# Gated unit begun before the attention layer ahead of it is finished, and an output bias added by VectorE

## The chip, the cores and the metric

The kernel runs on one core of a Trainium2 chip. The metric is the device time of one execution in microseconds (us). The core has five engines that run side by side and wait for one another through semaphores: TensorE (PE in the rows, its weight loads PEld), VectorE (DVE), ScalarE (ACT), GpSimd (POOL) and SyncE (SP), which here only issues DMAs. A name with a q (DVEq, PEldq, SPq) is the engine's sequencer.

## The reference, cut to what matters

Four layers work on a stream x of 2 batches x 512 tokens x 256 channels, in float32. Each layer adds a gated cross-attention and then a gated feed-forward part to x:

```python
x = x + tanh(g_xattn[l]) * attention_l(layernorm(x), ctx)      # l = 0..3
x = x + tanh(g_ffn[l]) * feed_forward_l(layernorm(x))
# attention of l = 2 and 3 ends with:   o @ Wo + bo
# feed-forward of l = 2, the gated unit:
h = silu(x @ w1 * s1) * (x @ w2 * s2)                          # 256 -> 1024
h = gelu(h @ h1 * sh1); h = gelu(h @ h2 * sh2)                 # 1024 -> 1024
out = h @ w3 * s3                                              # 1024 -> 256
```

Attention l = 1 has no biases. Feed-forward 1 is a mixture of 8 experts. The change is in attention 2 and 3 and in the gated unit.

## The kernel before, in words

The program is written engine by engine; each engine runs its list in order, and every dependence between engines is a `wait_ge` on a semaphore.

**Attention.** `schedule(l)` (line 144) writes one list of steps, which all engines walk through, each doing its own part. A group is two heads of one batch: 16 groups in layers 1 and 2, 8 in layer 3, the first half of them batch 0. A step "max" is a product whose row maximum VectorE takes (lines 1502 and 2217); "score" gives the transposed scores (L1521), which ScalarE turns into exponentials (L1176); "values" multiplies them with the values (L1536); "context" turns the sums back (L1555) and they are divided. The maxima run ahead of the scores, so near the end of a layer VectorE is through with them while TensorE and ScalarE still have scores to do. There batch 0 is finished: "heads" turns its context (L1563, one for every 128 channels: two in layer 2, one in layers 1 and 3), VectorE copies it out of PSUM (L2254), "out" multiplies two token tiles with Wo (L1574) and adds the bias bo by a product of a row of ones with the one row of bo (L1576), and VectorE adds that to x (L2261). Statistics (L1820, L1825), GpSimd's reciprocal deviation (L847, L848) and VectorE's normalisation (L1840) follow for batch 0. After the last scores "tokens" turns batch 0's normalised tiles (L1292), "heads" turns batch 1's context, ScalarE copies it (L1192), and "out" follows for batch 1. `bo` was replaced beforehand by bv @ Wo + bo (L1624, L1625, L1207).

**Between attention 2 and the gated unit.** TensorE runs 22 products that nobody reads (`hold_clock(LN_HOLDS[5], 2)`, L1283), then the transposes of batch 1 (L1292), then waits until ScalarE has copied them (`ln_evac`, L961). Two flags tell whether any weight of the unit needs a second float32r part; each of TensorE and VectorE reads them (`value_load`, L1778 and L2489) and branches (`If`, L1779, L2490, L2495). VectorE reads them right after its last maximum, and all its later steps of attention 2 stand within the two branches. There too it converts the unit's first two weight chunks (`split_weights`, L2443) behind the "out" steps, and splits the tokens of both batches in two float32r parts (`split_tokens`, L2420 and L2421).

**The gated unit** (`gated_unit`) is run once for batch 0 and once for batch 1. Its first layer has 8 blocks f of 128 channels: 8 products per block (L1729), ScalarE's silu (L1252), VectorE's multiplication (L2474) and conversion (L2476), GpSimd's low part (L932). Block f waits for the conversion of block f - 2 (`gated_high`). The second layer waits for the low parts of all blocks (`act_split`). The weights go by chunks over two buffers; SyncE loads a further chunk once VectorE has converted one (L584). Layer 3's attention follows, then the last feed-forward part, whose products begin with L1796.

## Time and profile before

| | us |
|---|---|
| median of 3 runs (lowest to highest) | 1114.46 (1112.02 to 1122.93) |
| the profiled execution, its own time | 1117.24 |
| its span, first to last instruction | 1115.5 |
| TensorE busy in it | 1015.7 |
| VectorE busy in it | 770.4 |
| mean granted clock of TensorE | 0.939 |

The span is what the trace covers; the execution's own time is 1.7 us longer. Busy time of TensorE counts an instruction at its modelled length, so it says that the engine had work and not that it ran at its best rate. The clock column gives the share of 2.4 GHz that TensorE was granted: 1.00 is 2.4 GHz and 0.50 is 1.2 GHz.

### The profile page before, as it was taken

The page shows a single profiled execution, that of the slowest core. Times are in us where ns is not written, and L with a number is a line of the kernel's source. Part 1 is how long each engine was busy: PE and PEld are TensorE (multiplying, and loading weights), DVE is VectorE, ACT ScalarE, POOL GpSimd, SP SyncE. Part 2 cuts the span into 40 slices and gives each one's busy share as a digit, 9 for nine tenths or more (in the row PEclk, how much of TensorE's full clock was granted, in tenths as well). Part 3 has the DMA queues.
Part 4 walks back from the last instruction along what each step waited for, and adds up shares of the span by engine and source line. Part 5 has one row for each costly group of instructions (what it writes and reads, how often), then busy time and mean ns, then how long its engine had stood idle before and what let it go on. Part 6 is the DMA issues. An engine that isn't in the chain of part 4 may idle for free.

```text
span 1115.5 us, 17599 instructions
## 1 busy us (share of the span) xinstructions
PE 1015.7 (91%) x6606; PEld 596.7 (53%) x6606; DVE 770.4 (69%) x1465; ACT 485.6 (44%) x704; POOL 287.3 (26%) x439
## 2 busy tenths in 40 slices
PE   8888975999999969995899999998989999899998
PEld 4323353544444446995454444444778787644445
DVE  5879868899999451453699999923545654799636
ACT  2553331477777700110157777732312212367542
POOL 3545700133433211003123443220400500114200
PEclk9889976999999968998999999969999999999889
DMA  6688912103330604985412241001254242100011
GB/s 208 216 280 277 354 31 65 40 24 110 116 91 13 171 28 165 357 323 144 139 40 65 50 122 44 24 2 38 95 170 132 95 140 72 35 12 13 2 29 38
DMA packets 79185, 121.86 MB, mean 109 GB/s; under 512 B 9733, under 2 KB 52904, under 8 KB 79090
## 3 DMA queue, kind: packets, MB, share of 16 engines
q1 hardware_dynamic: 59278, 79.29, 23.2%
q10 hardware_dynamic: 19044, 39.22, 10.1%
q0 software_dynamic: 768, 2.10, 0.6%
q8 instruction: 58, 0.95, 0.4%
q14 instruction: 37, 0.30, 0.1%
HBM read 92.10 MB, written 27.81 MB: 107 GB/s over the span
## 4 chain that ended last, share of the span: by engine, by line
PE 71%; DVE 20%; issue 4%; ACT 2%; POOL 1%; DMA 1%; SPq 0%; DVEq 0%; ACTq 0%; POOLq 0%
PE bank L1536 14%; PE bank L1502 14%; PE bank L1729 11%; DVE arena L2217 9%; PE st_bank L1656 4%; PE bank L1668 4%; PE st_bank L1521 3%; PE bank L1304 2%; PE st_bank L1729 2%; PE bank L1574 2%; PE st_bank L1454 1%; PE st_bank L1283 1%; PE st_bank L1292 1%; PE bank L1576 1%; PE bank L1555 1%
## 5 line engine op out<-in xcount | busy, mean ns | idle before, releaser
L2217 DVE TENSOR_REDUCE arena<-bank 128x1 f32<-128x512 f32 x640 | 396.8, 680 | 35.4 <-PE bank L1502 34.4
L1176 ACT ACTIVATE arena<-st_bank 128x1024 f32<-128x1024 f32 x320 | 312.2, 1022 | 155.4 <-PE st_bank L1521 154.4
L1502 PE MATMUL bank<-g_a 64*128 64x512 f32 x480 | 181.4, 477 | 11.4 <-DVE arena L2217 3.0
L1536 PE MATMUL bank<-arena,vaug 128*9 128x256 f32 (+2 forms) x2560 | 171.0, 385 | 2.0 <-ACT arena L1176 2.0
L1502 PEld LDWEIGHTS bank<-g_a 64*128 64x128 f32 x480 | 73.2, 183 | 124.5 <-DVE arena L2217 100.0
L1729 PE MATMUL bank<-g_a,g_w 128*128 128x512 f32 x512 | 119.3, 394 | 4.3 <-DVE g_w L2443 3.2
L1521 PE MATMUL st_bank<-g_a 64*128 64x512 f32 x480 | 117.4, 425 | 0.0
L1729 PEld LDWEIGHTS bank<-g_a,g_w 128*128 128x128 f32 x512 | 97.0, 190 | 25.9 <-DVE g_w L2443 3.6
L899 POOL COPY arena<-arena 8x32 f32<-8x32 f32 x160 | 32.1, 200 | 260.5 <-issue 137.0
L1536 PEld LDWEIGHTS bank<-arena,vaug 128*9 128x9 f32 (+2 forms) x2560 | 56.1, 92 | 77.4 <-issue 40.7
L1502 PE MATMUL bank<-g_x,g_a 64*128 64x512 f32 x160 | 63.5, 494 | 9.9 <-DVE arena L2217 3.6
L1521 PEld LDWEIGHTS st_bank<-g_a 64*128 64x128 f32 x480 | 63.2, 188 | 7.6 <-issue 4.2
L1254 ACT ACTIVATE arena<-bank,arena 128x512 f32<-128x512 f32 x32 | 22.0, 688 | 96.6 <-PE bank L1729 96.6
L2420 DVE CAST g_a<-arena 128x512 fp32r<-128x512 f32 x32 | 13.7, 427 | 65.6 <-ACT arena L1254 65.6
L847 POOL TENSOR_SCALAR rstd<-mv 128x4 f32<-128x4 f32 x16 | 3.8, 239 | 205.8 <-DVE mv L1825 205.8
L913 POOL TENSOR_TENSOR arena<-arena,minus_one 128x16 f32<-128x16 f32 x17 | 49.3, 2899 | 11.7 <-ACT arena L1169 11.7
L1217 ACT ACTIVATE arena<-st_bank 128x352 f32<-128x352 f32 x32 | 14.8, 464 | 85.8 <-PE st_bank L1656 85.8
L1502 PEld LDWEIGHTS bank<-g_x,g_a 64*128 64x128 f32 x160 | 26.1, 190 | 46.8 <-DVE arena L2217 32.6
L961 ACT ACTIVATE xnT<-st_bank 128x512 f32<-128x512 f32 x24 | 13.0, 594 | 85.8 <-PE st_bank L1292 85.8
L932 POOL TENSOR_TENSOR g_a<-arena,g_a 128x512 fp32r<-128x512 f32 x16 | 23.7, 1483 | 92.0 <-DVE g_a L2476 92.0
L1283 PE MATMUL st_bank<-identb 128*128 128x512 bf16 x149 | 40.5, 437 | 7.2 <-DVE arena L2330 5.0
L1656 PE MATMUL st_bank<-arena 128*128 128x176 f32 x256 | 41.2, 321 | 0.7 <-DVE arena L2346 0.7
(314 smaller groups left out, 1507.4 us busy)
## 6 DMA issues: line engine op xcount, KB each, us to landing
arena<-in_glu_w SPq DMA_DIRECT2D x39, 512.0 KB, 3.3
arena<-kv_table SPq DMA_DIRECT2D x11, 1024.0 KB, 7.9
ctxT<-in_glu_w ACTq DMA_DIRECT2D x22, 512.0 KB, 6.3
arena<-in_w SPq DMA_DIRECT2D x20, 512.0 KB, 6.0
kparts<-arena ACTq DMA_DIRECT2D x12, 512.0 KB, 5.1
arena<-in_w ACTq DMA_DIRECT2D x12, 512.0 KB, 3.6
xnT<-kv_table SPq DMA_DIRECT2D x5, 1024.0 KB, 6.9
g_a<-kparts SPq DMA_DIRECT2D x24, 192.0 KB
```

The costliest lines, as they stand in the source:

```text
L899: ch.link(pool.tensor_copy(mxq[0:HG * QT, r * SQ:(r + 1) * SQ], mxt[gi % 2][r * SQ:r * SQ + HG * QT, :]))
L913: ch.link(pool.tensor_tensor(rsum_p, sums[:, :, :, dh], bc(minus_one[:, 0:1].unsqueeze(2), [P, QT, 2 * HG]), ALU.pow))
L932: pool.tensor_tensor(g_a[0][1][:, f, :], g_tmp[f % 2], g_a[0][0][:, f, :].bitcast(F32), ALU.subtract).then_inc(act_split, 1)
L1176: act.activation(prob[sl % PROBS], st_bank[sl % 2][:], ACT.Exp, scale=scale).then_inc(exp_ready, 1)
L1283: pe.matmul(bank[b], identb[:], bc(identb[:].unsqueeze(1), [P, CH // P, P]), start=True, stop=True)
L1502: pe.matmul(bank[TURN_BANKS[place % 3]], Qc[gi % KQ_BUFS][rows, qt * P:(qt + 1) * P], Kc[gi % KQ_BUFS][rows, half * CH:(half + 1) * CH], s ...
L1521: ins = pe.matmul(st_bank[sl % 2][:, hh, :], Kc[gi % KQ_BUFS][rows, kt * P:(kt + 1) * P], Qc[gi % KQ_BUFS][rows, :], start=True, stop=True)
L1536: ins = pe.matmul(bank[7][at:at + dh + 1, 0:D], vaug[l][:, b * KT + 2 * m + i, h0 + hh, :], tiles[:, a], start=(m == 0 and i == 0), stop=( ...
L1656: ins = pe.matmul(bank[i % 4][:, f % UP_PER_BANK * CAP:(f % UP_PER_BANK + 1) * CAP], mw1[wbuf][:, c, f * P:(f + 1) * P], unit_inT[n % 2][: ...
L1668: ins = pe.matmul(bank[4 + n % 2][:, c * CAP:(c + 1) * CAP], mw2[wbuf][:, f, c * P:(c + 1) * P], hid[n % 2][:, f, :], start=(f == 0), stop ...
L1729: ins = pe.matmul(out, stationary, moving, start=(first and i == 0), stop=(last and i == len(pairs) - 1))
L2217: dve.tensor_reduce(mxh[gi % 2][:, col, hf:hf + 1], bank[TURN_BANKS[place % 3]], AX.X, ALU.max).then_inc(max_red, 1)
```

## The change

1. On VectorE the reading of the flags and the branch stand after batch 0 of attention 2 has been normalised, and no longer after the last maximum. In the branch stand, in this order: the first two weight chunks, the last context's division, `split_tokens(0)`, the "out" steps of batch 1, the statistics, block 0 of the unit, the normalisation of batch 1, block 1, and so on; `split_tokens(1)` stands behind block 3.
2. TensorE goes from the last "out" step straight to the unit's block 0, without the 22 holding products; the transposes of batch 1 stand ahead of block 3 and go to banks 4 and 5.
3. ScalarE copies batch 0's turned tokens ahead of the last "heads", loads the table of silu (by an activation of one element) before the unit, and copies batch 1's turned tokens ahead of block 3.
4. The bias: at the mixture's start TensorE spreads the two rows bo over 128 partitions, ScalarE multiplies them with tanh(g_xattn) into `bias_rows`, and in layers 2 and 3 VectorE adds that row to all of x (128x2048) behind batch 0's "heads" copies. The bias products of "out" are gone.

```diff
-LN_HOLDS = {3: 8, 4: 16, 5: 22, 7: 16}
+LN_HOLDS = {3: 8, 4: 16, 7: 16}
+SECOND_TOKENS_AT, SECOND_BANKS = 3, 2
...
@@ scalar, attention(l)
+                    elif step[0] == "tokens" and l == 2:
+                        ln_evac(2 * l + 1, [step[1]])
@@ scalar, ahead of the mixture
+            act.wait_ge(prepv_mm, NCT + 2)
+            for l in (2, 3):
+                ins = act.activation(bias_rows[:, l - 2], bank[3][:, (l - 2) * D:(l - 1) * D], ACT.Copy, scale=tgx[:, l:l + 1])
+            ins.then_inc(prepv_evac, 1)
@@ scalar, gated unit
-            ln_evac(5)
+            act.activation(exp_ready_table[:], onesf[0:1, 0:1], ACT.Silu)
...
+                if (h, layer, f) == (0, 0, SECOND_TOKENS_AT):
+                    ln_evac(5, [1], SECOND_BANKS)
@@ tensor, output
-                            ins = pe.matmul(o, xnT[0:n, c, t * P:(t + 1) * P], w[l]["o"][:, c, :], start=(c == 0), stop=(c == EC[l] - 1 and l == 1))
-                        if l > 1:
-                            ins = pe.matmul(o, onesf[0:1, :], w[l]["bo"][:], start=False, stop=True)
+                            ins = pe.matmul(o, xnT[0:n, c, t * P:(t + 1) * P], w[l]["o"][:, c, :], start=(c == 0), stop=(c == EC[l] - 1))
@@ tensor, the mixture's start
+            for l in (2, 3):
+                ins = pe.matmul(bank[3][:, (l - 2) * D:(l - 1) * D], onesf[0:1, :], w[l]["bo"][:], start=True, stop=True)
+            ins.then_inc(prepv_mm, 1)
...
+            pe.wait_ge(prepv_evac, NCT + 2)
             pe.wait_ge(slots_ready, 1)
@@ tensor, behind attention(2)
-            hold_clock(LN_HOLDS[5], 2)
-            ln_transposes(5, [1])
-            pe.wait_ge(xnT_ready, (LN_AT[5] + 1) * 4)
@@ tensor, gated_unit
+                            if (h, f) == (0, SECOND_TOKENS_AT):
+                                ln_transposes(5, [1], SECOND_BANKS)
...
+                        if (h, layer, f) == (0, 1, 0):
+                            pe.wait_ge(xnT_ready, (LN_AT[5] + 1) * 4)
@@ vector, attention(l)
+                        if l > 1 and c == EC[l] - 1:
+                            dve.wait_ge(prepv_evac, NCT + 2)
+                            ch.link(dve.tensor_tensor(x[:], x[:], bc(bias_rows[:, l - 2].unsqueeze(1), [P, NT, D]), ALU.add))
@@ vector, ahead of the branch
-            all_maxima = second.index(("shift", NGROUPS[2] - 1)) + 1
-            attention(2, second[:all_maxima])
+            first_done = second.index(("normalise", 0)) + 1
+            last_context = next(i for i, step in enumerate(second) if step[:2] == ("normal", NGROUPS[2] - 1)) + 1
...
+            attention(2, second[:first_done])
@@ vector, gated_unit
-                normalise(5, first=1)
+                attention(2, second[first_done:last_context])
                 split_tokens(0)
-                split_tokens(1)
+                attention(2, second[last_context:])
+                tile_statistics(5, NT - 1)
...
+                            if a == 1:
+                                normalise_batch(5, 1)
+                            if a == SECOND_TOKENS_AT + 1:
+                                split_tokens(1)
@@ vector, both branches
-                attention(2, second[all_maxima:])
                 gated_unit(True)
```

VectorE behind its last maximum of attention 2, before and after (STREAM_TRANSPOSE ends the maxima, COPY xnT is the "heads" copy of L2254):

```order
L2229 STREAM_TRANSPOSE arena<-arena 128x32 [waits max_lo,max_fin]
L2489 TENSOR_LOAD low_flags
L2489 ISA x2
L2489 TENSOR_LOAD low_flags
L2489 ISA x2
L2490 COMPARE_AND_BRANCH
L2254 COPY xnT<-bank 128x512 [waits ctxT_mm] x2
L2261 SCALAR_TENSOR_TENSOR x<-bank,tgx,x 128x512 [waits out_mm]
```

```order
L2241 STREAM_TRANSPOSE arena<-arena 128x32 [waits max_lo,max_fin]
L2266 COPY xnT<-bank 128x512 [waits ctxT_mm] x2
L2269 TENSOR_TENSOR x<-x,wo 128x2048 [waits prepv_evac]
L2276 SCALAR_TENSOR_TENSOR x<-bank,tgx,x 128x512 [waits out_mm,chain_dve]
```

The five rows of flags and branch left this place, and the 128x2048 addition (wo is the buffer of `bias_rows`) came behind the copies; flags and branch now stand behind the four normalisations of batch 0.

VectorE from batch 1's "out" steps on, after the change (CAST g_x and the TENSOR_TENSOR g_x behind it are `split_tokens`, L2496 and L2498 are a block's multiplication and conversion):

```order
L2276 SCALAR_TENSOR_TENSOR x<-bank,tgx,x 128x512 [waits out_mm]
L1832 BN_STATS bnst<-x 128x6 [waits x_ready] x3
L1837 BN_AGGR mv<-bnst 128x2 [waits chain_dve]
L1837 BN_AGGR mv<-bnst 128x2 x3
L2496 SCALAR_TENSOR_TENSOR arena<-st_bank,arena 128x512 [waits glu_act,glu_ld]
L2498 CAST g_a<-arena 128x512 [waits chain_dve]
L1852 TENSOR_SCALAR xn<-x,mv,rstd 128x256 [waits rstd_ready,var_ready]
L1852 TENSOR_SCALAR xn<-x,mv,rstd 128x256 x3
L2496 SCALAR_TENSOR_TENSOR arena<-st_bank,arena 128x512 [waits glu_act]
L2498 CAST g_a<-arena 128x512 [waits chain_dve]
```

Before, the two weight chunks, the normalisation and all four token splits stood between the statistics and block 0's multiplication; now the statistics are followed by block 0, and the normalisation stands between blocks 0 and 1.

TensorE from the last "out" step to the unit, before and after (L1737 is the unit's product of L1729):

```order
L1576 MATMUL bank<-bo,onesf 128x256
L1283 MATMUL st_bank<-identb 128x512 x22
L1292 MATMUL st_bank<-ident,xn 128x128 [waits xn_ready]
...
L1778 TENSOR_LOAD low_flags [waits xnT_ready]
...
L1779 COMPARE_AND_BRANCH
L1729 MATMUL st_bank<-g_x,g_w 128x512 [waits tokens_split,glu_split]
```

```order
L1584 MATMUL bank<-wo,xnT 128x256 [waits ctxT_ready]
L1584 MATMUL bank<-wo,xnT 128x256 x3
L1790 TENSOR_LOAD low_flags
...
L1791 COMPARE_AND_BRANCH
L1737 MATMUL st_bank<-g_x,g_w 128x512 [waits tokens_split,glu_split]
L1737 MATMUL st_bank<-g_x,g_w 128x512 x15
L1737 MATMUL st_bank<-g_x,g_w 128x512 [waits gated_high,tokens_split,glu_split]
L1737 MATMUL st_bank<-g_x,g_w 128x512 x7
L1302 MATMUL bank<-ident,xn 128x128 [waits xn_ready]
```

The 22 holding products are gone, and the transposes of batch 1 moved from ahead of the unit to behind its block 2.

## Rows read from the trace of the kernel before

**Rows 1.** The page: busy time, share of the span and instructions of each engine.

```profile
PE 1015.7 (91%) x6606; PEld 596.7 (53%) x6606; DVE 770.4 (69%) x1465; ACT 485.6 (44%) x704; POOL 287.3 (26%) x439
```

**Rows 2.** Chain of waits, 722 to 800 us: start us, us, what.

```profile
726.30 0.21 DVE arena L2229
...
727.62 2.76 issue
...
731.81 2.08 PE bank L1574 x4
...
761.05 1.09 ACT xnT L1192 x2
...
763.94 1.06 PE bank L1574 x4
765.00 0.62 PE bank L1576 x2
...
769.11 0.75 DVE x L2261
...
770.52 1.19 DVE g_w L2443 x2
...
772.93 1.05 POOL rstd L848
...
774.08 1.38 DVE xn L1840 x4
...
787.12 0.70 ACT arena L1252
787.84 0.76 DVE arena L2474
788.63 0.44 DVE g_a L2476
...
799.44 1.67 POOL g_a L932
```

**Rows 3.** Stretches: start:end, length, busy us (instructions) by engine, TensorE's clock, DMA.

```profile
369.70:373.20 3.50, 3.50 (x29) 1.85 (x27) 1.18 (x2) 1.94 (x3) 3.23 (x3) 1.00 0.05 5
1052.00:1063.00 11.00, 11.00 (x56) 5.12 (x54) 3.60 (x11) 3.07 (x3) 3.95 (x4) 0.53 0.01 2
731.90:748.00 16.10, 16.10 (x48) 7.96 (x48) 3.29 (x10) 2.05 (x2) 0.74 (x3) 0.50 0.00 0
```

**Rows 4.** Timelines of DVE and PE, ends of attention 1 and 3: start, length, instruction, idle.

```profile
368.41 0.21 DVE L2229 STREAM_TRANSPOSE arena<-arena 128x32 f32<-128x32 f32 x1
386.00 0.66 PE L1555 MATMUL bank<-ident,xnT 128*128 128x128 f32 x4 [0.50 <-ACT xnT L1188]
1049.31 0.21 DVE L2229 STREAM_TRANSPOSE arena<-arena 128x32 f32<-128x32 f32 x1
1073.49 0.66 PE L1555 MATMUL bank<-ident,xnT 128*128 128x128 f32 x4 [0.50 <-ACT xnT L1188]
```

**Rows 5.** Timeline of PE, attention 2's last context and the unit's first products.

```profile
758.89 0.66 PE L1555 MATMUL bank<-ident,xnT 128*128 128x128 f32 x4 [0.50 <-ACT xnT L1188]
...
778.58 5.52 PE L1729 MATMUL st_bank<-g_x,g_w 128*128 128x512 f32 x16 [2.63 <-DVE g_x L2421]
784.99 3.96 PE L1729 MATMUL st_bank<-g_x,g_w 128*128 128x512 f32 x16 [0.89 <-DVE g_a L2476]
...
801.15 26.18 PE L1729 MATMUL bank<-g_a,g_w 128*128 128x512 f32 x114 [0.55 <-POOL g_a L932]
```

**Rows 6.** Lines L2421 and L2368, all instructions: min/median/max ns.

```profile
L2421 DVE TENSOR_TENSOR g_x<-xnT,g_x x4: 691/692/692, 775.8 to 779.0; 128x512 fp32r<-128x512 f32 x4
L2368 DVE TENSOR_TENSOR ctxT<-ctxT x21: 1212/1225/1227, 443.5 to 508.4; 128x1024 int32<-128x1024 int32 x21
```

**Rows 7.** Chain of waits, end of attention 3; then PE's timeline at the mixture's start.

```profile
1078.56 0.43 PE bank L1576 x2
...
415.62 12.40 PE L1283 MATMUL st_bank<-identb 128*128 128x512 bf16 x44 [4.97 <-DVE arena L2330]
```

More of the change, by code:

```diff
@@ L342, in build @@
         exp_ready_table = sb("exp_ready_table", [1, 1])
+        bias_rows = wo0[:]
         chain_dve, chain_act, chain_pool = sem("chain_dve"), sem("chain_act"), sem("chain_pool")
@@ L956, in _, with ln_evac @@
             ch = Chain(act, chain_act)
-            def ln_evac(stage, halves=range(2)):
+            def ln_evac(stage, halves=range(2), first=0):
                 for i in (h * DC + c for h in halves for c in range(DC)):
@@ L960, in ln_evac @@
                     act.wait_ge(xnT_mm, LN_AT[stage] * 4 + i + 1)
-                    act.activation(xnT[:, c, h * CH:(h + 1) * CH], bank[i], ACT.Copy).then_inc(xnT_ready, 1)
+                    act.activation(xnT[:, c, h * CH:(h + 1) * CH], bank[first + i], ACT.Copy).then_inc(xnT_ready, 1)
             def ctx0_evac(b):
@@ L1291, in transposes @@
                     for c in range(ec):
-                        ins = pe.transpose(bank[(t // QT) * ec + c][0:n, (t % QT) * P:(t % QT + 1) * P], src[:, t, c * P:c * P + n], ident[:])
+                        ins = pe.transpose(bank[base + (t // QT) * ec + c][0:n, (t % QT) * P:(t % QT + 1) * P], src[:, t, c * P:c * P + n], ident[:])
                         if t % QT == QT - 1:
@@ L1443, in _, with ln_transposes @@
             i8_products(0)
-            def ln_transposes(stage, batches=range(B)):
-                transposes(xn, xnT_mm, 0, D, xn_ready, XN0[stage], batches)
+            def ln_transposes(stage, batches=range(B), first=0):
+                transposes(xn, xnT_mm, first, D, xn_ready, XN0[stage], batches)
             def query_product(l, j, parts=range(DC)):
@@ L2495, in _ @@
             with dve.If(no_low):
-                attention(2, second[all_maxima:])
                 gated_unit(False)
```

1 line of the change is left out of this document (added).

## The prediction

> **What bounds the kernel now.** I read the page first: TensorE is busy for 91% of the span and VectorE for 69% [rows 1]. An engine as full as that gains from what it no longer does, from what it no longer waits for, and from its clock. So next came the chain of waits around the change, 722 to 800 us, then the clock of stretches, then the timelines. They show three things.
>
> First, behind its last maximum (the transpose at 726.30) VectorE does not copy batch 0's context, although that is turned; the branch stands in between, and 2.76 us go by in which nothing is waited for [rows 2]. TensorE's first output product starts only at 731.81. From 731.90 to 748 TensorE is busy all the time, but at 1.2 GHz, clock 0.50 [rows 3]: four products with Wo take 2.08 us, and 1.06 us in batch 1, at full clock [rows 2]. Layer 1 has the same transition without branch and without bias, and its clock stays at 1.00 [rows 3].
>
> Second, between the last output product (over at 769.1) and the unit's steady rhythm TensorE does nothing that counts: holding products, transposes of batch 1, then 2.63 us of waiting for VectorE's token split, then two blocks at a lower rate (5.52 us where the next two take 3.96) [rows 5]. VectorE's own work in that stretch (weights, statistics, normalisation, splits) is a chain that nothing covers [rows 2].
>
> Third, the second layer starts at 801.15, when GpSimd has made the last low part [rows 2, 5]; from there TensorE runs almost without a gap. Whatever earlier start that point gets moves all that is behind it.
>
> **Part A, the end of attention 2.** From the last transpose of maxima to the turning of the last context: 758.89 - 726.30 = 32.6 us in layer 2 [rows 2, 5], but 386.00 - 368.41 = 17.6 in layer 1 [rows 4], with the same number of groups. The changed layer 2 differs from layer 1 in one more "heads" (about 0.6 with its copy) and in 8 more products with Wo, 2 x 1.06 = 2.1 [rows 2]. That makes 20.3, so A gives 32.6 - 20.3 = 12.3 us: the stall, the biases (four at half clock) and the half clock itself. It holds only if the clock stays up, as in layer 1. VectorE reads the flags later, in time in which it waits for the last context: it normalises batch 0 some 13 us behind the copies, loads and branch take 4, the two weight chunks 1.2, and the last context comes 20.3 us behind the transpose. About 2 us are left over; if they were not enough, the excess would be paid in full.
>
> The branch is the first place where I weigh a page. The row shows 2.76 us between the branch and the next work [rows 2]. The Trainium skill (Advanced Engine Details and Errata, Control Flow Timing) gives a compare-and-branch about 108 ns. By the page, moving it would return almost nothing and A would be some 2.7 us smaller; the measurement decides, and I keep the row.
>
> **Part B, batch 1's output.** Four bias pieces of 0.62 us go [rows 2]: 2.5 us. ScalarE now copies the turned tokens before the turned context. The two context copies took 1.09 us and started as soon as TensorE had turned the first half; the token copies are two of the same size and can start some 0.65 us earlier, so the context is late by about 0.45. B = 2.05 us.
>
> **Part C, from the last output product to the second layer.** Before: 801.15 - 769.1 = 32.0 us. After, counted from the end of the output products (time 0), with 1.98 us for a block [half of 3.96, rows 5], 0.70 for silu, 0.76 and 0.44 for multiplication and conversion [rows 2]:
> TensorE does blocks 0 and 1 from 0 to 4.0. VectorE finishes output and statistics at 2.3 (from 769.11 to GpSimd's row at 772.93, less the chunks' 1.19 and 0.3 for its shorter first instruction [rows 2]); GpSimd's deviation is there 1.4 later. Block 0 is converted at 4.0, normalisation (1.38) ends at 5.4, block 1 is converted at 6.6, a weight chunk ends at 7.3. Block 2 runs 4.1 to 6.1, the 8 transposes to 7.0, block 3 from 7.0 to 9.0, block 4 to 11.0, block 5 from 11.1 to 13.1. VectorE converts block 3 at 10.95, a weight chunk ends at 11.65, and then `split_tokens(1)` takes 2 x (0.42 + 0.69) = 2.2 (0.69 [rows 6]), to 13.85. Only then does block 4's multiplication come, converted at 15.1, for which block 6 waits: TensorE idles 2.1 us. Blocks 6 and 7 end at 19.2, silu and VectorE at 21.2, GpSimd's low part (1.67 [rows 2]) at 22.9. C = 32.0 - 22.9 = 9.1 us. Its parts: the wait and the holding products 9.5, the silu table that is loaded ahead 1.3, the slow first blocks 1.6, less transposes 0.9 and the new stall 2.1; they make 9.4, near enough. Queued behind `split_tokens(1)` on VectorE are the multiplications of blocks 4 to 7, and TensorE waits for them through the conversions; behind the normalisation it is block 1's multiplication, which costs nothing because block 2's product covers it.
>
> **Part D, the end of attention 3.** The same stretch lasts 1073.49 - 1049.31 = 24.2 us [rows 4]; with layer 1's 17.6 (one "heads", one set of products, as in layer 1) the most to gain is 6.6. There the clock falls without any stall: 0.53 from 1052 to 1063 [rows 3], behind output products with 32 rows and biases with one. If it still falls, only the four biases go, 0.43 each at full clock [rows 7] and twice that for the two at half: 2.6 us. Nothing in the trace shows products of 32 rows without the biases between them. I take the middle, 4.6, and keep both ends.
>
> **Part E, layer 3's last output.** Four biases of 0.43 us [rows 7] = 1.7, of which VectorE's two additions and the holding products behind them may keep some; bounds 0 and 1.7, taken 1.3.
>
> **Costs taken as nothing.** The addition to x over 2048 columns stands in no row. 512 columns take 0.69 us and 1024 take 1.22 [rows 6], so 0.53 per 512 more: 2.3 us; bounds 1.2 and 4 x 0.69 = 2.8. In layer 2 it lies in the 2.8 us between the copies and the end of the first output step. In layer 3 the first addition of output starts 0.9 us behind its product, but no later than before, and its bank is wanted three turns on. The spreading of the bias (four products of one row, about 2.1 us at half clock, two small activations) lies in the 4.97 us that TensorE waits for VectorE ahead of the 44 holding products [rows 7]; bounds 0 and 0.5, since a load of ScalarE's queue goes out 4 us later.
>
> **Sum.** 12.3 + 2.05 + 9.1 + 4.6 + 1.3 = 29.4 us. Against the execution's own time: 1117.24 - 29.4 = 1087.9. The median of the runs is 2.8 us lower, which gives 1085.1. I say 1086.5.
>
> **Rivals.**
> 1. The clock falls inside the unit. VectorE's queue makes TensorE idle for 2.1 us at block 6, and a wait of 2.63 us together with transposes stood ahead of the slow blocks [rows 5]. For it: that row; against it: the new idle time has dense products on both sides. Price once: 5.52 - 3.96 = 1.6, twice 3.2. Time 1088 to 1090. This is also where the Trainium skill speaks against the change (TensorE: Matmul & The Clock Gate, Part 4, PE-mode transpose): transposes do not count as busy time for the clock. By that rule the eight transposes that now stand within the blocks, followed by the wait at block 6, pull the clock down. In attention 2's last part the rows of before show transposes with the clock still at 1.00 afterwards (1.06 us for four products at 763.94 [rows 2]), which neither proves nor refutes it.
> 2. Attention 2's output of batch 0 stays at half clock: the stall was not the reason, the transposes ahead of it were. Then 4.2 us of products with Wo, 0.9 of scores and 1.0 to 1.4 of values are paid twice, A shrinks by 6.5, and the time is 1093. Against it: layer 1.
> 3. VectorE becomes the bound of the unit's first layer: normalisation, splits and chunks are only moved, and each second block waits for product and silu (2.7 us) as block 0 does. VectorE's own work behind the last product is about 18.3 us; with 4 x 2.7 that is 29.1 instead of 22.9: C is 2.9, time 1093. If all eight wait, 39.9, and 1103.5: the early start is given back whole.
> 4. Slower than before. Half clock can last under full load: 16.1 us of it with TensorE busy throughout [rows 3]. If the many small waits of the unit's first layer leave TensorE at 1.2 GHz for the first batch's pass, its 16 us of blocks and 16 x 16 dense products at 0.23 us (26.18 / 114 [rows 5]) = 59 us are paid twice: 1086.5 + 75 = 1161. It decides from 29.4 us of dense work at half clock on, about 128 products. Against it: at 784.99 the clock was back, four blocks' time after the unit's start [rows 5].
> That the change does not do what it says would be case 3 in its whole form.
>
> **How the numbers follow.** Forecast (own range 1080 to 1089, by D's ends of +-2 and some 2 us of run to run difference) 0.62; rival 1, 0.13; rival 2, 0.11; rival 3, 0.11; rival 4, 0.03. What a measurement of this kernel can tell from no change is about 1%, 11 us. The range 1079 to 1097 takes in the forecast, rivals 1 and 2 and the near form of rival 3, and leaves out the far form of rival 3 and rival 4. Faster by over 1% (under 1103.3): 0.95; within 1%: 0.02, from the far end of rival 3; slower: 0.03.
>
> **What would show it.** Right: the first product with Wo of attention 2's batch 0 about 3 us behind the last transpose of maxima and at clock 1.00; 20 us from that transpose to the last context's turning; the unit's first block directly behind the last output product, 4.0 us for two; one gap of about 2 us ahead of block 6; 23 us from the last output product to the second layer; 18 to 22 us for the stretch in layer 3; an addition over 2048 columns of 2.3 us, twice. Wrong: a clock of 0.50 in the first 16 us behind the transpose, gaps ahead of most blocks, the last context's division waiting for the branch, or the unit's dense products at 0.43 us each.

## The result, and the profile after

| | before | after |
|---|---|---|
| median of the runs beside each other (lowest to highest) | 1114.05 (1112.02 to 1122.93) | 1084.69 (1080.08 to 1086.85) |
| the profiled execution, its own time | 1117.24 | 1080.08 |
| its span | 1115.5 | 1078.3 |
| TensorE busy | 1015.7 | 985.0 |
| VectorE busy | 770.4 | 776.8 |
| mean granted clock | 0.939 | 0.956 |

The ratio of the times is 0.9716, with a 95% interval from 0.9655 to 0.9777. The median is 29.4 us lower, and the sum on record said 29.4. That agreement is partly luck: one term was 2.9 us too large, the other four were too small by 0.5 to 1.9, and part of the gain belongs to something that the kernel before does in some executions and not in others. One run of this study, of e6 below (1121.30 us at a clock of 0.848), was a slow one and is left out of its median and ratio.

To compare, I cut each execution at the same six instructions: VectorE's last transpose of maxima in attention 2 (the last of that layer), TensorE's turning of the last context, VectorE's last addition of attention 2's output, the first product of the unit's second layer behind GpSimd's last low part, the last transpose of maxima in attention 3, the turning of its last context, and the end of the span. A, B, C, M, D, E are the stretches between them. Here are A to C in the chain of waits of the changed kernel, columns as in [rows 2]:

```profile
723.99 1.92 PE bank L1584 x8
725.91 0.43 PE st_bank L1531
726.34 1.93 PE bank L1584 x8
...
740.24 0.66 PE bank L1565 x4
740.90 0.78 PE st_bank L1302 x7
741.70 1.09 ACT xnT L963 x2
742.78 0.99 ACT xnT L1196 x2
743.82 3.73 PE bank L1584 x16
747.65 0.75 DVE x L2276
...
751.65 2.34 DVE xn L1852 x4
...
759.88 1.44 DVE g_x L2437
...
764.37 5.34 PE st_bank L1737 x16
...
771.75 1.67 POOL g_a L934
773.46 2.60 PE bank L1737 x10
```

The last transpose of maxima stands at 720.64, so A is 740.24 - 720.64 = 19.6 us. The "issue" piece of [rows 2] (time in which VectorE waits for nothing that the profile shows) is gone from the chain, eight products with Wo take 1.92 us (at half clock four took 2.08), and the unit's products follow the last output directly. Against [rows 3], the windows of the same two stretches read, in the changed kernel:

```profile
724.00:740.00 16.00, 15.09 (x146) 7.39 (x146) 7.46 (x17) 10.38 (x13) 3.82 (x4) 1.00 0.12 37
762.00:764.30 2.30, 0.00 (x0) 0.00 (x0) 2.23 (x6) 0.18 (x1) 0.00 (x1) 0.92 0.24 96
764.40:770.00 5.60, 5.60 (x19) 4.48 (x20) 3.21 (x5) 0.95 (x2) 2.96 (x3) 0.74 0.28 97
1021.00:1038.00 17.00, 15.94 (x164) 6.90 (x162) 7.42 (x16) 12.50 (x16) 8.33 (x9) 1.00 0.01 1
```

The columns are the stretch, its length, busy time of PE, PEld, DVE, ACT and POOL with their instructions, the granted clock, the DMA share and GB/s. The first and the last row show the end of attention 2 and of attention 3 at full clock. The two rows between show the price inside the unit: TensorE has nothing to do for 2.3 us of this window while VectorE is busy for 2.23 of them, and in the 5.6 us behind it the clock is 0.74.

The timeline of the changed kernel, first where VectorE reads the flags, then in the unit (start, duration, instruction, in brackets the idle time ahead of it and what ended it):

```profile
736.30 1.30 DVE L2460 CAST g_w<-arena 128x1024 fp32r<-128x1024 f32 x2 [2.86 <-issue]
740.94 0.26 DVE L2250 RECIPROCAL arena<-bank 128x16 f32<-128x16 f32 x1 [3.34 <-PE bank L1565]
...
751.59 1.29 POOL L934 TENSOR_TENSOR g_a<-arena,g_a 128x512 fp32r<-128x512 f32 x1
751.65 2.34 DVE L1852 TENSOR_SCALAR xn<-x,mv,rstd 128x256 f32<-128x256 f32 x4
...
755.17 6.28 PE L1737 MATMUL st_bank<-g_x,g_w 128*128 128x512 f32 x24 [0.55 <-DVE g_a L2498]
...
759.35 1.68 POOL L934 TENSOR_TENSOR g_a<-arena,g_a 128x512 fp32r<-128x512 f32 x1 [0.82 <-DVE g_a L2498]
...
759.79 1.52 DVE L2437 CAST g_x<-xnT 128x512 fp32r<-128x512 f32 x1
...
761.95 0.42 DVE L2437 CAST g_x<-xnT 128x512 fp32r<-128x512 f32 x1
...
764.37 5.33 PE L1737 MATMUL st_bank<-g_x,g_w 128*128 128x512 f32 x16 [2.91 <-DVE g_a L2498]
...
773.46 1.90 PE L1737 MATMUL bank<-g_a,g_w 128*128 128x512 f32 x7 [0.55 <-POOL g_a L934]
```

The 2.86 us of the branch are still there, but VectorE then waits another 3.34 us for the last context, so nobody waits for it. The gap ahead of block 6 is 2.91 us (2.1 were forecast), and the two blocks behind it take 5.33 us and not 3.96. Of two equal conversions in the token split, the one that begins 0.44 us behind a subtraction of GpSimd takes 1.52 us, and the one without such a neighbour 0.42. The normalisation, which took 1.38 us before [rows 2], takes 2.34 beside another such subtraction.

### The profile page after: what moved, and what is told of

It reads as the page before. It is cut to its first block, busy times and chain, and to the rows that moved or that the text cites. A ratio compares the mean times of both kernels' runs of the same rounds, so it can differ in the third digit from the quotient of the medians.

```text
span 1078.3 us, 17505 instructions
## 1 busy us (share of the span) xinstructions
PE 985.0 (91%) x6556; PEld 582.9 (54%) x6556; DVE 776.8 (72%) x1467; ACT 486.8 (45%) x707; POOL 290.1 (27%) x439
## 4 chain that ended last, share of the span: by engine, by line
PE 70%; DVE 21%; issue 4%; ACT 2%; POOL 2%; DMA 1%; SPq 0%; POOLq 0%; DVEq 0%; ACTq 0%
PE bank L1546 14%; PE bank L1512 14%; PE bank L1737 12%; DVE arena L2229 9%; PE st_bank L1667 4%; PE bank L1679 4%; PE st_bank L1531 3%; PE bank L1314 2%; PE st_bank L1737 2%; PE st_bank L1464 1%; PE bank L1584 1%; PE st_bank L1302 1%; PE bank L1565 1%; DVE bnst L1832 1%; DVE arena L1961 1%
## 5 line engine op out<-in xcount | busy, mean ns | idle before, releaser
L1546 PE MATMUL bank<-arena,vaug 128*9 128x256 f32 (+2 forms) x2560 | 168.5, 381 | 2.0 <-ACT arena L1178 2.0
L1737 PE MATMUL bank<-g_a,g_w 128*128 128x512 f32 x512 | 117.7, 390 | 4.3 <-DVE g_w L2460 3.2
L1531 PE MATMUL st_bank<-g_a 64*128 64x512 f32 x480 | 115.2, 417 | 0.0
L1737 PEld LDWEIGHTS bank<-g_a,g_w 128*128 128x128 f32 x512 | 95.8, 188 | 25.5 <-DVE g_w L2460 3.6
L901 POOL COPY arena<-arena 8x32 f32<-8x32 f32 x160 | 34.7, 217 | 257.9 <-issue 137.1
L1512 PEld LDWEIGHTS bank<-g_x,g_a 64*128 64x128 f32 x160 | 26.1, 191 | 45.8 <-DVE arena L2229 31.9
L881 POOL MEMSET g_a<- 2x512 f32 x56 | 28.9, 516 | 46.5 <-PE st_bank L1531 44.2
```

Source lines behind the costliest of these rows:

```text
L881: ins = pool.memset(Qc[gi % KQ_BUFS][h * HALF_P:h * HALF_P + SHIFT_ROWS].bitcast(F32), 0.0)
L901: ch.link(pool.tensor_copy(mxq[0:HG * QT, r * SQ:(r + 1) * SQ], mxt[gi % 2][r * SQ:r * SQ + HG * QT, :]))
L1512: pe.matmul(bank[TURN_BANKS[place % 3]], Qc[gi % KQ_BUFS][rows, qt * P:(qt + 1) * P], Kc[gi % KQ_BUFS][rows, half * CH:(half + 1) * CH], s ...
L1531: ins = pe.matmul(st_bank[sl % 2][:, hh, :], Kc[gi % KQ_BUFS][rows, kt * P:(kt + 1) * P], Qc[gi % KQ_BUFS][rows, :], start=True, stop=True)
L1546: ins = pe.matmul(bank[7][at:at + dh + 1, 0:D], vaug[l][:, b * KT + 2 * m + i, h0 + hh, :], tiles[:, a], start=(m == 0 and i == 0), stop=( ...
L1737: ins = pe.matmul(out, stationary, moving, start=(first and i == 0), stop=(last and i == len(pairs) - 1))
```

## The experiments

Twelve runs were made beside the pair above: eight altered kernels (e1 to e8) and four repeats (c1 to c4). This table has the stretches of each in its profiled execution, in us, from the starts of the rows named above, and the median of its timed executions with the ratio to the kernel before, timed beside it on the same chip (there its median was 1109.55 to 1114.05). For the three kernels whose second layer starts without a gap behind a low part, C and M are given as their sum.

| kernel | A | B | C | M | D | E | median | ratio (95% interval) |
|---|---|---|---|---|---|---|---|---|
| before | 32.6 | 10.2 | 32.0 | 248.2 | 24.2 | 42.0 | 1114.05 | |
| c2, before again | 24.8 | 10.2 | 31.7 | 246.9 | 19.4 | 42.1 | 1102.81, one run | |
| c3, before a third time | 32.8 | 10.2 | 32.0 | 248.1 | 24.2 | 42.1 | 1111.69, one run | |
| e1, branch only | 22.5 | 10.2 | 32.9 | 248.2 | 19.4 | 41.7 | 1101.04 | 0.9915 (0.9881 to 0.9949) |
| e2, bias only | 23.5 | 7.1 | 32.7 | 246.5 | 17.7 | 40.1 | 1092.12 | 0.9838 (0.9811 to 0.9864) |
| c4, bias only again | 23.4 | 7.1 | 32.9 | 246.9 | 17.7 | 40.2 | 1097.23, one run | |
| e3, changed, no bias part | 22.5 | 10.5 | 26.0 | 248.2 | 19.4 | 42.0 | 1091.94 | 0.9839 (0.9803 to 0.9876) |
| changed | 19.6 | 7.4 | 25.8 | 246.9 | 17.7 | 40.2 | 1084.69 | 0.9716 (0.9655 to 0.9777) |
| c1, changed again | 19.6 | 7.4 | 25.9 | 247.9 | 17.7 | 40.2 | 1083.21 | 0.9749 (0.9712 to 0.9786) |
| e8, no table ahead | 19.6 | 7.4 | 27.1 | 246.9 | 17.7 | 40.1 | 1083.40 | 0.9753 (0.9718 to 0.9789) |
| e4, late token split | 19.6 | 7.4 | 21.7 | 248.0 | 17.7 | 40.2 | 1079.19 | 0.9715 (0.9686 to 0.9743) |
| e5, low parts left out | 19.6 | 7.4 | C + M 273.7 | | 17.7 | 40.3 | 1083.28 | 0.9735 (0.9698 to 0.9773) |
| e6, last low part by VectorE | 19.6 | 7.4 | C + M 269.2 | | 17.7 | 40.1 | 1078.11 | 0.9695 (0.9662 to 0.9727) |
| e7, third layer's weights | 19.6 | 7.4 | C + M 262.3 | | 17.7 | 40.2 | 1071.08 | 0.9642 (0.9609 to 0.9675) |

A to E agree within 0.1 to 0.3 us wherever nothing was changed and the clock was the same. What lies ahead of A does not: the last transpose of maxima in attention 2 stands between 719.7 and 728.4 us over these kernels, although hardly anything before it differs. Most of this spread arises early: attention 1's last transpose of maxima already stands between 362.9 and 370.7 us. That is why the profiled pair differs by 37.2 us and the medians by 29.4: 726.30 - 720.64 = 5.7 us came from ahead of the change. For terms of one or two microseconds the stretches are the better measure, and the times serve for the sums.

**Branch alone (e1) and bias alone (e2).**

```diff
-            all_maxima = second.index(("shift", NGROUPS[2] - 1)) + 1
+            all_maxima = second.index(("normalise", 0)) + 1
```

> The kernel before, with VectorE's reading of the flags and its branch moved behind the normalisation of attention 2's batch 0, and nothing else: the bias products, the holding products and the whole way into the unit stay. Theory (the stall takes the clock down in attention 2): the four products with Wo of batch 0 take 1.06 us and no longer 2.08, the stretch from the last transpose of maxima to the last context's turning falls from 32.6 to 22 to 23 us, layer 3 stays at 24.2 us, and the time is about 1104 us. Rival (the bias products take it down, as they may in layer 3): the clock still reads about 0.5 from 732 to 748, only the stall of 2.76 us goes, the stretch lasts 29 to 30 us and the time is about 1111.

In e2 the kernel before takes the whole of point 4 of the change, with the same lines as the diff shown above, and nothing of points 1 to 3:

```diff
+                        if l > 1 and c == EC[l] - 1:
+                            dve.wait_ge(prepv_evac, NCT + 2)
+                            ch.link(dve.tensor_tensor(x[:], x[:], bc(bias_rows[:, l - 2].unsqueeze(1), [P, NT, D]), ALU.add))
...
-                        if l > 1:
-                            ins = pe.matmul(o, onesf[0:1, :], w[l]["bo"][:], start=False, stop=True)
```

> The kernel before, with the output bias added by VectorE in attention 2 and 3 (the rows spread at the mixture's start, the bias products gone), and nothing else: flags and branch, holding products and the way into the unit stay. Theory (two separate causes): the stall of 2.76 us stays and takes attention 2's clock down as before, so that its stretch falls from 32.6 only to about 29.5 us; batch 1's output gains 2.5, and layer 3's stretch goes from 24.2 to 17.6 because its clock stays at 1.00, its last output gains 1.3 to 1.8. Time about 1100 us. Rival (the biases alone take down the clock in attention 2): its stretch falls to about 23 us and the time is about 1094. Rival for layer 3 (its clock held in the changed kernel for another reason): its stretch stays at 21.6 us or more and the time is about 1104.

The first output products in e1's timeline, then in e2's:

```profile
728.02 1.13 PE L1574 MATMUL bank<-wo,xnT 128*128 128x256 f32 x4
729.08 0.69 PE L1576 MATMUL bank<-bo,onesf 1*128 1x256 f32 x2
729.71 1.13 PE L1574 MATMUL bank<-wo,xnT 128*128 128x256 f32 x4
```

```profile
733.82 3.54 PE L1579 MATMUL bank<-wo,xnT 128*128 128x256 f32 x8 [2.12 <-DVE xnT L2261]
737.82 1.99 PE L1579 MATMUL bank<-wo,xnT 128*128 128x256 f32 x8
751.80 0.66 PE L1560 MATMUL bank<-ident,xnT 128*128 128x128 f32 x4 [0.50 <-ACT xnT L1189]
```

Without the stall (e1) the products run at full clock with the biases between them. With the stall and without the biases (e2) the first eight products take 3.54 us where the next eight take 1.99, and then the clock is back. So in these two profiles either half of the change, alone, avoids the 16 us at half clock. e1's stretch A is the one that the theory has. e1 has D at 19.4 us, though, where its expectation said 24.2, and a time 3 us lower. e2 gives A as the rival has it (23.5 us) and D as the theory has it (17.7), and a time near the rival's.

The two parts do not add up. Put first, the bias part gives 1 - 0.9838 = 1.6%, 18 us. Put last, on top of e3, it gives 0.9839 - 0.9749 = 0.9%, 10 us. The 8 us between are, as far as the stretches tell, the two low clocks: from the first profile of before to e2 A loses 9.1 us and D 6.5, from e3 to c1 only 2.9 and 1.7. They count for whichever part comes first.

**The changed kernel without the bias part (e3).** The product of the biases is back in "out", and the two additions to x are taken out.

> The changed kernel with the bias products back and VectorE's two additions to x taken out (the spreading of the rows stays, and nobody reads them). Theory (branch and bias are separate causes, the stall alone took attention 2's clock down): attention 2's stretch is 20 + 2.5 = about 22.5 us at clock 1.00, batch 1's output 2.5 us longer, layer 3's stretch back at about 24 us with a clock near 0.53 in part of it, its last output 1.3 to 1.8 longer: 1084.7 + 2.5 + 2.5 + 6.5 + 1.5 = about 1098 us. Rival (one-row products at the end of attention 2 take the clock down without a stall, as they may in layer 3): 6 us more, about 1104.

The stretch A was 22.5 us, as the theory has it, and B 10.5. D was 19.4 us and not 24: the time came out 6 us under the theory's. That D says that the low clock of layer 3, on which half of my term D rested, does not come with the biases alone. e1 has the same 19.4. So the kernel before had to be profiled again.

**The kernel before again (c2, c3), and bias alone again (c4).**

> The kernel before once more, unaltered, profiled to see which of its low clocks come back. Theory (the half clock of attention 2 belongs to the program: a stall and one-row products behind it; that of layer 3 was one execution's, since it did not appear with the same biases in the branch-only kernel and the one without the bias part): attention 2's stretch is about 32.6 us again with a clock near 0.50, layer 3's is 19.4 us and not 24.2. Rival (both belong to the program): 32.6 and 24.2. Rival (both are chance): 22 to 26 and 19.4.

> The kernel before a third time, with the same expectations: attention 2's stretch 32.6 us if its half clock belongs to the program, layer 3's 19.4 us if its low clock was one execution's.

> The kernel with the bias part alone once more, unaltered. Theory (without the one-row products the clock comes back after four products behind the stall): attention 2's stretch 23.5 us again. Rival (that was one execution's luck): up to 29.5 us, with products of 2.08 us per four.

Windows of c2 (first row) and of c3 (the other two), the columns as above:

```profile
732.00:748.00 16.00, 16.00 (x130) 7.63 (x132) 4.76 (x14) 8.85 (x10) 1.34 (x3) 1.00 0.01 2
```

```profile
726.50:742.50 16.00, 16.00 (x48) 7.86 (x48) 3.29 (x10) 2.05 (x2) 0.45 (x3) 0.50 0.00 0
1045.00:1056.00 11.00, 11.00 (x50) 5.86 (x52) 3.29 (x10) 3.41 (x5) 4.15 (x5) 0.59 0.01 2
```

The same program, with the same stall (2.18 us ahead of the first output product in c2, 2.37 in c3), ran through those 16 us once at 1.00 with 130 products, and once at 0.50 with 48. Both falls came together: in the first profile and in c3 attention 2 and layer 3 are slow, in c2 neither is. No theory of mine had that. In the eleven profiles of the other kernels, each of which lacks the stall or the biases or both, neither fall appears; c4 repeats what e2 showed (A 23.4 us, the first eight products in 3.42 us behind a stall of 2.31), so the short loss of clock behind the stall came in both profiles of that kernel. The times point the same way for more executions. Without the falls the kernel before should be 17.3 us above the changed one (from c2's stretches: A 5.2, B 2.8, C 5.8, D 1.7, E 1.8), but its medians lie 28 to 29 us above. So most executions probably have the falls, which together cost 32.7 - 24.8 + 24.2 - 19.4 = 12.7 us. For e1 the stretches ask for 2.9 + 2.8 + 7.0 + 0.3 + 1.7 + 1.5 = 16.2 us over c1, and its median is 17.8 above c1's. For e3 they ask for 9.9, and its median is 8.7 above. That leaves no room for 12.7 more in most of their executions. For single executions only the profiles tell, and the kernel before has three, e1 and e3 one each.

**What happens in the unit (e4).** Batch 1's token split goes out of the first layer and into the second, a half behind each of two blocks:

```diff
-                            if a == SECOND_TOKENS_AT + 1:
-                                split_tokens(1)
+                            if a in (NF + 1, NF + 2):
+                                split_tokens(1, [a - NF - 1])
```

> The changed kernel with batch 1's token split taken from between blocks 3 and 4 of the unit's first layer and done in two halves behind the second and the third block of its second layer, where VectorE waits 1.87 us per block. Theory (VectorE's queue makes TensorE wait at block 6, and this wait takes the clock down for the two blocks behind it): the gap of 2.91 us ahead of block 6 falls under 0.6 us, blocks 6 and 7 take 3.96 us and not 5.33, the second layer starts 21 to 22.5 us behind the last output product's addition and not 25.8, no wait appears in the second layer, and the time is about 1080.7 us (4 less than the changed kernel). Rival (the eight transposes within the blocks take the clock down, the wait does not): the blocks behind them still run at a lower clock, and the gain is about 2.6 us, 1082. Rival (the second layer has no room): its blocks become longer than 3.63 us and the gain is given back, 1085.

e4's timeline, and its window over the same blocks:

```profile
758.62 1.04 PE L1302 MATMUL bank<-ident,xn 128*128 128x128 f32 x8
760.19 10.46 PE L1737 MATMUL st_bank<-g_x,g_w 128*128 128x512 f32 x40 [0.54 <-DVE g_a L2498]
770.49 3.36 PE L1737 MATMUL bank<-g_a,g_w 128*128 128x512 f32 x14
774.41 5.96 PE L1737 MATMUL bank<-g_a,g_w 128*128 128x512 f32 x25 [0.56 <-POOL g_a L934]
```

```profile
760.00:770.00 10.00, 9.74 (x38) 6.93 (x39) 7.50 (x13) 3.43 (x6) 7.38 (x5) 1.00 0.31 105
```

Blocks 3 to 7 are one run of 40 products at clock 1.00. The gap of 2.91 us and the slow blocks are gone, C is 25.8 - 21.7 = 4.1 us shorter, and the median is 4.0 under c1's (ratios 0.9715 and 0.9749). Of C's 4.1 us, M gave back 0.1 to 1.1, which is what M also does between executions of one kernel; the second layer has room for the split. The eight transposes still stand in the middle of the blocks (758.62). The rule of the Trainium skill that I had weighed against the change (TensorE: Matmul & The Clock Gate, Part 4, PE-mode transpose) did not decide here: with the transposes and without the wait, no clock is lost. Whether transposes make a wait worse stays open (e5, below).

**Why the conversions are long (e5).** GpSimd's low parts are cut from 512 columns to 4. The low parts of the first layer's output are so left out, and the buffer is set to zero once.

```diff
+                    pool.wait_ge(glu_split, 2)
+                    ch.link(pool.memset(g_a[0][1][:].bitcast(F32), 0.0))
...
-                            pool.tensor_tensor(g_a[0][1][:, f, :], g_tmp[f % 2], g_a[0][0][:, f, :].bitcast(F32), ALU.subtract).then_inc(act_split, 1)
+                            pool.tensor_tensor(g_a[0][1][:, f, 0:4], g_tmp[f % 2][:, 0:4], g_a[0][0][:, f, 0:4].bitcast(F32), ALU.subtract).then_inc(act_split, 1)
```

> The changed kernel with GpSimd's low parts of the unit's first layer cut from 512 columns to 4 (the low parts of that layer's output are left out: the rest of them is set to zero once, ahead of the unit). Theory (VectorE's conversions and normalisation are lengthened because GpSimd's subtraction holds something that both need): the conversion in the token split takes 0.43 and not 1.52 us, the normalisation 1.38 and not 2.34, the gap ahead of block 6 falls from 2.9 to about 1.8 us, and with the last low part gone (1.66) the second layer starts 2.5 us earlier in the first pass and 1.5 in the second: about 4 us less than the changed kernel, 5.4 if the clock also stays up behind block 6. Rival (they are long for a reason of their own, such as the wait for their semaphores): 1.52 and 2.34 us stay, and only 2 x 1.5 = 3 us go.

e5's timeline:

```profile
752.56 3.71 POOL L932 MEMSET g_a<- 128x4096 f32 x1
752.60 0.69 ACT L1264 ACTIVATE arena<-st_bank,arena 128x512 f32<-128x512 f32 x1 [1.11 <-PE st_bank L1739]
752.95 2.10 PE L1739 MATMUL st_bank<-g_x,g_w 128*128 128x512 f32 x8 [0.39 <-DVE g_a L2500]
752.95 4.42 DVE L1854 TENSOR_SCALAR xn<-x,mv,rstd 128x256 f32<-128x256 f32 x4
...
764.68 0.42 DVE L2439 CAST g_x<-xnT 128x512 fp32r<-128x512 f32 x1
...
768.15 5.51 PE L1739 MATMUL st_bank<-g_x,g_w 128*128 128x512 f32 x16 [1.80 <-DVE g_a L2500]
```

As to the cause, the theory holds, and my own addition shows it best. The zeroing of 3.71 us fell on the normalisation, which took 4.42 us: it ended 757.37 - 756.27 = 1.10 us behind the zeroing, the time of three of its four pieces (1.38 / 4 = 0.35 each). So the first had, it seems, been held until GpSimd was through. With GpSimd idle the conversion takes 0.42 us and the gap is 1.80 us, as expected. These rows fit VectorE's instructions within SBUF waiting for the whole of GpSimd's, and not the two sharing. The Trainium skill says so (SBUF — State Buffer, Who interferes with whom): a copy, a cast or a tensor_scalar of VectorE in its fast modes takes a port pair that GpSimd also uses, and the later of the two waits for the whole of the other. The trace agrees. As to the time the expectation failed: nothing was gained, since the late normalisation cost what the low parts gave back, and the clock fell behind a gap of 1.80 us as it does behind 2.91 (5.51 us for two blocks). Earlier in e5 the eight transposes came late, between waits of 1.42 and 0.68 us, and the two blocks behind them took 5.50 us as well; in e8 (below) a wait of 1.66 us without transposes took no clock. Two single places don't tell whether the transposes or the length of the waits makes that difference.

**The last low part by VectorE (e6), and the third layer's weights (e7).** e6 is e4 with

```diff
+                                if f == NF - 1:
+                                    dve.wait_ge(gated_high, a // BLOCKS * NF + NF)
+                                    dve.wait_ge(act_split, a)
+                                    dve.tensor_tensor(g_a[0][1][:, f, :], g_tmp[a % 2], g_a[0][0][:, f, :].bitcast(F32), ALU.subtract).then_inc(act_split, 1)
```

and GpSimd's loop one block shorter. e7 is e6 with another place for the two chunks of w3, each converted at once behind the chunk that precedes it:

```diff
-GLU_ORDER = GLU_HALF[:-NF] + [W3_FIRST + i for i in range(W3_CHUNKS)] + GLU_HALF[-NF:] + GLU_HALF
+GLU_ORDER = GLU_HALF[:-NF - 1] + [W3_FIRST, GLU_HALF[-NF - 1], W3_FIRST + 1] + GLU_HALF[-NF:] + GLU_HALF
...
-                    if n + 2 < len(GLU_ORDER):
-                        split_weights(n + 2, low_weights)
+                        if converted < len(GLU_ORDER):
+                            split_weights(converted, low_weights)
+                            converted += 1
+                        while converted < len(GLU_ORDER) and GLU_ORDER[converted] >= W3_FIRST:
+                            split_weights(converted, low_weights)
+                            converted += 1
```

> The kernel with the late token split, and in each pass the low part of the first layer's last block made by VectorE (0.69 us from the last conversion on) in place of GpSimd (1.66 us from 0.5 us behind it). Theory (that low part alone sets the start of the second layer): it starts about 1.0 us earlier in each pass, and the time is 2 us under that of the late token split, about 5 to 6 under the changed kernel. Rival (a product or the silu ends last there): no difference from the late token split, about 3 to 4 under the changed kernel.

> The kernel of the last low part by VectorE, and the two chunks of the fourth matrix (w3) converted one each behind the last blocks but two of the second layer, so that the third layer's first chunk no longer waits behind both. Theory (the idle time of 3.17 us ahead of the third layer is VectorE's queue of conversions, and the slower products behind it, in some executions, come from that idle time): the gap falls under 0.5 us, the third layer's first eight products run at 1.00 in every case, and the time is 3.2 to 4.8 us under the kernel of the last low part by VectorE. Rival (the chunk's load or the last low part of the second layer ends just as late): 0 to 1 us less.

TensorE from the second layer into the third, in e6 and then in e7:

```profile
800.04 12.12 PE L1737 MATMUL bank<-g_a,g_w 128*128 128x512 f32 x45 [3.17 <-DVE g_w L2460]
```

```profile
784.40 27.82 PE L1738 MATMUL bank<-g_a,g_w 128*128 128x512 f32 x122
```

e6 gave 0.6 us of C + M and not 2, and its median lies 1.1 us under e4's, which is within the spread of either: the gap ahead of the second layer was only 0.55 us in each pass (773.46 above), and it can give back no more than that. I had counted how much sooner the low part is there, and not how long anybody waited for it. In e7 the gap of 3.17 us is gone, and with it the slow products behind it (45 in 12.12 us, 0.269 each, against 27.82 / 122 = 0.228): 3.17 + 45 x 0.041 = 5.0 us. In all, C + M is 6.9 us shorter. Of the other 1.9, 1.8 lie at the start of attention 3: its first part takes 13.9 us in e6, where the clock reads 0.50 from 931.4 to 935.4, and 12.1 in e7, where the same products run at 1.00. The two profiles of the changed kernel differ there in the same way (13.9 and 12.2 us), so these 1.8 us are not shown to be e7's gain. The median is 7.0 under e6's, more than the 3.2 to 4.8 expected, and 12.1 under c1's: e7 beats the kernel before and the changed one.

**The table of silu (e8).** The activation of one element ahead of the unit is taken out. c1, the control for these kernels, ran as it had been expected to:

> The changed kernel once more, unaltered, as the measure for the three kernels beside it and for what differs from run to run: about 1083 us, 28 to 30 less than the kernel before. Theory (the way into the unit is the same in every execution): from the last maximum's transpose in attention 2 to the turning of the last context 19.6 us, from the last addition of output to the second layer 25.8 us with a gap of 2.9 us ahead of block 6 and a lower clock behind it. Rival (the lower clock behind block 6 was one run's): blocks 6 and 7 take 3.96 us here. The first 200 us may differ by up to 7 us.

> The changed kernel without the activation of one element that loads silu's table ahead of the unit. Theory (the table load of 1.28 us then stands ahead of block 0's silu and everything behind it on VectorE moves by it): from the last addition of output to the second layer 27.1 us and not 25.85, time 1.3 us more than the changed kernel. Rival (the load is hidden beside the wait for block 0, or taken up by the gaps of TensorE in the unit's first layer): 25.9 to 26.3 us, no difference in the time.

c1's blocks 6 and 7 took 5.43 us behind a gap of 2.90, so the lower clock there is the program's own. e8's timeline:

```profile
752.04 1.28 ACT L1261 ACT_TABLE_LOAD   x1 [5.72 <-PE st_bank L1736]
```

```profile
755.48 2.10 PE L1736 MATMUL st_bank<-g_x,g_w 128*128 128x512 f32 x8 [1.66 <-DVE g_a L2497]
```

The load now stands ahead of block 0's silu, and TensorE waits 1.66 us ahead of block 2 and not 0.39. C is 27.05 - 25.85 = 1.2 us longer, as the theory has it. In the times (0.9753 against 0.9749) a microsecond cannot be seen.

## Why the prediction was right, and where its steps were not

- **A (12.3 forecast).** Shown, with a better division than mine. In the executions that fall, A goes from 32.6 or 32.8 to 19.6: 13.0 to 13.2 us. I had ascribed the half clock to the stall. In the profiles the long fall comes only where stall and one-row products are both there (not in e1 and e3, which lack the stall, nor in e2 and c4, which lack the products), and even then not in every execution (c2). Without it A gives 24.8 - 19.6 = 5.2 us: 2.3 for the stall (c2 to e1), 2.9 for the biases (e1's 22.5, and e3's, to 19.6). The row of 2.76 us was the right one to go by: where it stood in the way the branch cost 2.3 us (with all that was moved beside it); in the changed kernel "issue" still lasts 2.86 us and lies in the wait for the last context, which VectorE enters with 3.34 us to spare. The trace of before says more about the branch than my row did:

```profile
L2490 DVEq COMPARE_BRANCH  x1: 56/56/56, 727.6 to 727.6; - x1
L2495 DVEq COMPARE_BRANCH  x1: 50/50/50, 730.4 to 730.4; - x1
```

The flags are read by 727.5, and the branch instruction itself lasts 56 ns. The 2.76 us lie between it and the next `If`, that is, on the way past the first body, which is not executed. TensorE, whose executed body stands first (L1779, 80 ns), starts its next weight load 0.14 us behind its branch. Whether the other order of the two bodies would save VectorE's 2.76 us too was not run. The 108 ns that the Trainium skill gives for a compare-and-branch (Advanced Engine Details and Errata, Control Flow Timing) are near what these rows show for the instruction, and not for the way behind it.

- **B (2.05).** 10.2 to 7.4 = 2.8. ScalarE's order cost 0.28 (1.02 us idle ahead of the output products, before 0.74), less than my 0.45. The biases gave 3.1 and not 2.5: with a bias behind each, the token tiles follow each other every 1.69 us (728.02 to 729.71 in e1), without it every 3.73 / 4 = 0.93, so a bias costs 0.76 and not its own 0.62.
- **C (9.1).** This is the term that was wrong: 32.0 to 25.8 is 6.2 us. The ladder of the prediction is right up to block 2 (4.0 us). Then the normalisation takes 2.34 us and not 1.38, block 1 is converted 0.9 later and block 3 starts at 7.5 and not 7.0; the first conversion of the token split takes 1.1 us more than its row of before; block 6 starts at 16.7 and not 15.2; and its two blocks are 1.4 us slow. The failed step is that durations were taken from a place where GpSimd is idle and used for one where it subtracts; that makes 1.5 of the 2.9 us by which the term was too large, and the lower clock of the two blocks makes the other 1.4. Rival 1, the clock at block 6, came in as the cheap one of its two forms (1.6 forecast, 1.4 measured) and goes when the wait goes, with the transposes left in place (e4).
- **D (4.6, with ends 2.6 and 6.6).** 24.2 to 17.7 = 6.5 against the profiled execution, so near the upper end; 1.7 of it is the four biases, and 4.8 a low clock that the kernel before has in two of its three profiles. The lower end rested on a clock that stays low without the biases, which came in none of nine profiles without them; but with biases and no fall (c2, e1, e3) the gain is 1.7, under my lower end.
- **E (1.3).** 42.0 to 40.2 = 1.8, the four biases in full.
- **Taken as nothing.** The addition to x took 2.28 us (2.3 estimated) and lies beside scores and transposes. The bias rows at the mixture's start cost nothing that shows: from attention 1's last transpose of maxima to attention 2's it is 726.30 - 368.41 = 357.9 us before and 720.64 - 363.51 = 357.1 after.
- **The sum.** 13.0 + 2.8 + 6.2 + 6.5 + 1.8 = 30.3 for a fallen execution of before, and 17.3 for one like c2. The medians differ by 28.5 to 29.4.
- **Rivals 2, 3 and 4** did not come. In the changed kernel no gap ahead of a block of the first layer passes 0.55 us outside block 6, and the two blocks behind block 6's gap cost 1.4 to 1.6 us more than at full clock, in its two profiles and in e3's and e8's. The largest loss in the unit is another one, which the kernel before has too: the 128 products behind the 3.17 us ahead of the third layer took 29.3 us in the changed kernel's first profile, 31.9 in c1 and 32.2 in e3, against 29.2 in e7, without the gap.

## What to carry to other kernels

A gain that is a clock belongs to several parts of a change at once and cannot be added up part by part; profile the kernel before more than once ahead of putting a low clock in the sum. When work is moved between engines' idle times, take its duration from a row with the same neighbours, and put what has slack where its engine waits anyway: the token split cost 4 us more in the first layer than in the second. A branch costs the time until its engine is at work again, and not what the instruction lasts: read both. What a faster step returns is the gap that ends on it, not the time that the step itself saves.

## What the runs showed of the hardware

- One program, two courses: with a stall of 2.2 to 2.4 us and one-row products behind it, the next 16 us ran at clock 1.00 in one execution and at 0.50 in two, with TensorE busy throughout in each. The low clock 320 us later, in layer 3, came in those same two executions alone. What ties them together stays open.
- In products of the unit, a gap of 2.9 us (four profiles) or 1.8 us (one) was followed by two blocks of 5.3 to 5.5 us in place of 3.96. Gaps of 0.4 to 0.55 us, and two of 1.66 us (e8, and e2 ahead of its blocks 2 and 3), had no slow products behind them. Behind the 3.17 us ahead of the third layer the loss over 128 products changed from execution to execution, from 0.1 us (changed) to 3.0 (e3).
- VectorE's conversion of 512 columns took 1.52 us beside GpSimd's subtraction and 0.42 without, and four normalisations 4.42 us beside a zeroing of 3.71, 2.34 beside a subtraction of 1.29, and 1.38 with GpSimd idle.
- A compare-and-branch of VectorE past a body that is not executed lasted 56 ns, and 2.76 us went by until its next instruction (2.71 in the changed kernel); TensorE's, into the body that follows it, lasted 80 ns, and a weight load began 0.14 us behind it.
- Almost the same instructions up to attention 2's last transpose of maxima took 719.7 to 728.4 us. 7.8 of these 8.6 us of spread are there at attention 1's, and the traces compared here name no cause.
